# A POOL fill and a wait on its signal behind every gather of a graph convolution

## The chip, the cores and the metric

One Trainium2 chip, one core. The metric is the device time of one execution in microseconds (us); the kernel before takes 2434.01 us (median of 3 runs, 2430.92 to 2440.19).

## What is computed

One edge convolution over a graph of 6250 nodes with 64 channels and 200,000 edges sorted by destination, then a residual and a layer norm. In the reference, cut:

```python
mean = jnp.mean(x, axis=0)
var = jnp.mean(jnp.square(x - mean), axis=0)
xn = (x - mean) * rsqrt(var + 1e-5) * gamma + beta
feat = jnp.concatenate([xn[dst], xn[src] - xn[dst]], axis=-1)
h = relu(feat @ W1 + b1)            # 200000 x 128
msg = h @ W2 + b2                   # 200000 x 64
agg = segment_max(msg, dst, 6250)   # 0 where a node has no edge
agg = relu(jnp.where(isfinite(agg), agg, 0.0))
out = layernorm(x + agg)            # over the 64 channels
```

## The kernel before

The first layer is linear, so it is split over the two ends of an edge: a table `a_dram` holds each node's share as a destination and `b_dram` (128 floats a node) its share as a source. The edges are cut in two halves that run side by side, each in 196 steps of 512 edges (`NI = 196`, `GE = 512`). The sources' rows come in two ways. For 28 steps (`picked`) PE selects them by matmuls with one-hot matrices (`select`, L1146 and L1153), whose tiles are spread over all steps, and DVE makes the one-hots (`node_onehot`, L919). For the other 168 steps POOL gathers them with indirect DMAs of 128 rows each, eight to a step (four tiles, two halves): for the first 12 such steps 64 channels out of `x` (`gather`, L494; the first one needs four), 92 gathers, and for 156 steps 128 channels out of `b_dram` (`gather_wide`, L511), 1248 gathers.

What orders the work is written out by hand: each engine has its own program, and semaphores tie them together.

- POOL: a few constants (L478 to L486; L480 waits for L478's signal), then the 92 narrow gathers back to back, then the wide ones. The first wide one waits until `b_dram` is written. Wide gathers go into a ring of eight buffers (`NXB = 8`): group i waits for `wide_ps`, the signal that PE has transposed group i - 8; groups 2 to 7 wait for `x_ps`, since they lie where the narrow rows lay. At the end POOL scatters the last rows of the output (L526).
- PE, in step k of the loop: transposes of the running maxima of step k - 2 (`turn`, L1196, signal `turn_ps`), the gathered rows of the step (`rows_wide`, L1205, signal `wide_ps`), the destination's share (`hidden_dst`, L1215), the messages of step k - 1 (L1190), the sums of step k - 2 (L1234), then some tiles of the selection.
- ACT: takes what `turn` left out of PSUM (`take_rows`, L683, waits for `turn_ps`), the hidden layer's relu (L688), one-hots of the windows (L640, L644).
- DVE: picks of rows (L972, waits for `turn_ps`), one-hots for the selection (L919), the running maximum over each segment (L993, waits for PE L1190).
- SP: loads of keys and tables, stores.

Before the loop PE makes the tables (L1094), ACT and DVE split and store them (L596, L602, L826, L832), and SP writes them out.

Of the kernel before, what the change touches and what calls it, by code (L numbers as in the profile page):

```python
# [6 lines left out]
def edge_conv_program(nc, x, src, dst, gamma, beta, W1, b1, W2, b2, out):  # L7
# [13 lines left out]
    P = 128  # L21
# [66 lines left out]
    def wide_slot(i):  # L88
        return (i + NX // 2) % NXB
# [4 lines left out]
    def sides(k):  # L94
        return 1 if k == 0 else 2

    def landed(g):
        return 16 * TG * sides(gathered[g])
# [11 lines left out]
    with ctx:  # L110
        def sb(name, shape, dt=f32):
            return ctx.enter_context(nc.sbuf_tensor(name, shape, dt))
# [4 lines left out]
        def sem(name):  # L117
            return ctx.enter_context(nc.semaphore(name))
# [69 lines left out]
        cen_sq = sb("cen_sq", [P, C])  # L188
        nrm = sb("nrm", [P, 5])
        yblk = sb("yblk", [P, C])  # L190

        src_tv = src_t[:, :].rearrange("p (h b e) -> p h b e", h=2, b=NB)
        src_b = src_t[0:PN, 0:2 * GE]
# [96 lines left out]
        acc_ps, added = sem("acc_ps"), sem("added")  # L290
        end_step, end_sq, end_std, xwin_used = sem("end_step"), sem("end_sq"), sem("end_std"), sem("xwin_used")
        y_ready, y_out, tail_out = sem("y_ready"), sem("y_out"), sem("tail_out")

        g_in, g_pair_in, g_x_ps, g_x_sb = sem("g_in"), sem("g_pair_in"), sem("g_x_ps"), sem("g_x_sb")
        g_hid_ps, g_hid_sb, g_msg_ps, g_msg = sem("g_hid_ps"), sem("g_hid_sb"), sem("g_msg_ps"), sem("g_msg")
# [18 lines left out]
        def edge_tiles(eng, body):  # L314
            with eng.Fori(0, E // P) as i:
                body(i, i * P)
            if E % P:
                body(E // P, E - P)

        @block.sync  # L320
        def _(sp):
# [74 lines left out]
            def starts(ap, last):  # L396
                _, firsts = nc.values_load_multi_w_load_instructions(
                    ap, engines=[mybir.EngineType.SP], min_val=0, max_val=last,
                    skip_runtime_bounds_check_because="in_order is set only where every start lies in 0..last")
                return firsts  # L400
# [75 lines left out]
        @block.gpsimd  # L476
        def _(pool):
            pool.memset(ident[:, :], 0.0).then_inc(consts_ready, 1)  # L478
            pool.wait_ge(consts_ready, 1)
            pool.affine_select(out=ident[:, :], in_=ident[:, :], compare_op=ALU.not_equal, fill=1.0, base=0,  # L480
                               pattern=[[-1, P]], channel_multiplier=1).then_inc(consts_ready, 1)
            pool.iota(slot_row[:, :], pattern=[[1, SL]], base=1, channel_multiplier=0,
                      allow_small_or_imprecise_dtypes=True).then_inc(consts_ready, 1)
            pool.iota(slot_rep[:, :], pattern=[[1, SL], [0, NPC]], base=1, channel_multiplier=0,
                      allow_small_or_imprecise_dtypes=True).then_inc(consts_ready, 1)
            pool.iota(part_col[:, :], pattern=[[0, 1]], base=0, channel_multiplier=1,  # L486
                      allow_small_or_imprecise_dtypes=True).then_inc(consts_ready, 1)

            def gather(g):
                k = gathered[g]  # L490
                b, q = divmod(k * TG, SB)
                for t in range(TG):
                    for h in range(sides(k)):
                        pool.indirect_dma_start(xs[:, g, t, h, :], None, x[:, :],  # L494
                                                bass.IndirectOffsetOnAxis(ap=src_ix[:, b, q + t, h:h + 1], axis=0))\
                            .then_inc(rows_in[g], 16)

            def gather_wide(i):
                k = gathered[NX + i]
                u = wide_slot(i)  # L500
                if i == 0:
                    pool.wait_ge(b_first, 32)
                    pool.wait_ge(b_out, 32 * (AG - 1))
                if i >= NXB:
                    pool.wait_ge(wide_ps, i - NXB + 1)
                elif i >= NXB - NX // 2:
                    pool.wait_ge(x_ps, 2 * u + 2)
                b, q = divmod(k * TG, SB)
                for t in range(TG):
                    for h in range(2):  # L510
                        pool.indirect_dma_start(xb[:, u, t, h, :], None, b_dram[:, :],  # L511
                                                bass.IndirectOffsetOnAxis(ap=src_ix[:, b, q + t, h:h + 1], axis=0))\
                            .then_inc(wide_in[u], 16)

            pool.wait_ge(src_ix_ready, 2)
            for g in range(NX):
                gather(g)
            pool.wait_ge(flag_ready, 1)
            windowed = pool.value_load(in_order[0:1, 0:1], min_val=0, max_val=1)
            with pool.If(windowed == 1):  # L520
                pool.wait_ge(src_ix_ready, 5)
                for i in range(len(gathered) - NX):
                    gather_wide(i)

                def scatter(p):
                    pool.indirect_dma_start(out[:, :], bass.IndirectOffsetOnAxis(ap=tail_ix[0:ROWS, p:p + 1], axis=0),  # L526
                                            y[:, p, :], None, bounds_check=N - 1, oob_is_err=False).then_inc(tail_out, 16)

                pool.wait_ge(tail_ready, 1)
                pool.wait_ge(y_ready, LB // WB + 1)  # L530
                pool.wait_ge(y_out, 32 * LB)
                for p in range(WB - 2):
                    scatter(p)
                for p in range(WB - 2, WB):
                    pool.wait_ge(y_ready, len(GROUPS) - WB + p + 1)
                    scatter(p)
            with pool.Else():
                for u in range(NX):
                    pool.wait_ge(rows_in[u], landed(u))

                def edge_tile(i, first):
                    loaded = pool.to_reg(i * 48 + 48)
                    pool.wait_ge(src_ix_ready, 2)
                    pool.wait_ge(g_in, loaded)
                    for side in range(2):
                        pool.indirect_dma_start(pair[:, side, :], None, x[:, :],
                                                bass.IndirectOffsetOnAxis(ap=pair_ix[:, side:side + 1], axis=0)).then_inc(g_pair_in, 16)

                edge_tiles(pool, edge_tile)
# [787 lines left out]
```

## Time and profile before

| | us |
|---|---|
| median of 3 runs | 2434.01 |
| span of the profiled execution | 2422.7 |
| PE matmul busy in it | 1818.5 (75%) |
| DVE busy | 1292.7 (53%) |
| POOL busy | 1283.2 (53%) |
| ACT busy | 862.0 (36%) |
| mean granted TensorE clock | 0.878 |

The span runs from the first to the last instruction of the profiled execution; the page gives no other time of its own for that execution. A busy engine in these rows has an instruction running; time in which it waits for a signal is idle. In a timeline a bracket behind an instruction says how long its engine had been idle and what ended that; "remote" or "unknown queue" means that no instruction ends at the time of the signal. A gather on POOL ends in these rows when its descriptors are written, not when the rows have landed.

### The profile page before, as it was taken

What the parts mean: (1) busy time and instruction counts of PE and PEld (TensorE: products, weight loads), DVE (VectorE), ACT (ScalarE), POOL (GpSimd) and SP (SyncE); (2) the same over time, 40 slices, a digit from 0 to 9 for tenths busy, and PEclk for the clock granted to TensorE, in tenths of its full rate; (3) what the DMA queues carried; (4) which work ended last, traced back from release to release, by engine and by line L of the source; (5) the groups of instructions that cost most, each with busy time, mean ns of one, the idle gap of its engine ahead of it and who ended that gap; (6) DMA issues with size and microseconds to landing.
All of it is one profiled execution on the core that took longest, in us unless ns stands there. A gap on an engine that the chain in (4) does not pass through costs nothing.

```text
span 2422.7 us, 31826 instructions
## 1 busy us (share of the span) xinstructions
PE 1818.5 (75%) x12305; PEld 938.5 (39%) x12305; DVE 1292.7 (53%) x2070; ACT 862.0 (36%) x968; POOL 1283.2 (53%) x1356
## 2 busy tenths in 40 slices
PE   2046887787878778787878878878788778887785
PEld 1032444343434434343434444444444434444443
DVE  2054655565555555555555556556456555565553
ACT  2044443333333333333333333333334333333333
POOL 7715245556555565456555565555655565555621
PEclk6557899998999999898989899998999988898996
DMA  4154223233333332333323333233323333333320
GB/s 93 35 173 122 59 84 81 77 90 86 80 86 84 88 95 70 85 81 96 87 70 91 87 87 80 81 89 95 89 72 94 91 81 81 75 94 87 76 62 5
DMA packets 132832, 202.31 MB, mean 84 GB/s; under 512 B 74828, under 2 KB 76937, under 8 KB 132648
## 3 DMA queue, kind: packets, MB, share of 16 engines
q0 software_dynamic: 43440, 85.03, 16.5%
q1 hardware_dynamic: 87946, 115.04, 14.9%
q8 instruction: 97, 1.59, 0.3%
q10 hardware_dynamic: 1294, 0.20, 0.1%
q14 instruction: 55, 0.45, 0.1%
HBM read 189.19 MB, written 12.60 MB: 83 GB/s over the span
## 4 chain that ended last, share of the span: by engine, by line
another core or an unknown queue 38%; PE 29%; ACT 19%; issue 8%; DVE 5%; DMA 1%; SPq 0%; POOLq 0%; DVEq 0%; ACTq 0%
PE ps_g L1146 10%; PE ps_g L1153 6%; ACT hid L688 5%; ACT best L640 5%; PE ps_mr L1190 4%; ACT best L644 4%; ACT best L683 3%; PE ps_acc L1234 2%; DVE oh L919 2%; PE ps_h L1205 2%; PE ps_mr L1196 2%; PE ps_h L1215 1%; DVE runmax L993 1%; PE ps_h L1222 1%
## 5 line engine op out<-in xcount | busy, mean ns | idle before, releaser
L511 POOL DMA_INDIRECT xb<-b_dram,src_ix x1248 | 1181.1, 946 | 1031.4 <-PE ps_h L1205 384.9
L919 DVE TENSOR_SCALAR oh<-ps_k 128x1024 bf16<-128x1024 bf16 x1372 | 849.6, 678 | 1.0
L1146 PE MATMUL ps_g<-oh,xtab 128*128 128x512 bf16 x2744 | 643.5, 387 | 5.8 <-issue 5.0
L1190 PE MATMUL ps_mr<-hid,w 128*64 128x512 f32 x784 | 270.8, 776 | 369.9 <-ACT best L683 325.6
L972 DVE TENSOR_TENSOR best<-ps_acc,last_key 128x336 f32<-128x336 f32 x196 | 99.3, 507 | 815.8 <-remote 655.9
L683 ACT ACTIVATE best<-ps_mr 128x512 f32<-128x512 f32 x196 | 117.0, 597 | 1097.1 <-remote 816.3
L1146 PEld LDWEIGHTS ps_g<-oh,xtab 128*128 128x128 bf16 x2744 | 256.9, 99 | 375.6 <-issue 103.3
L1153 PE MATMUL ps_g<-oh,xtab 128*64 128x512 bf16 x2744 | 387.1, 424 | 12.6 <-issue 11.3
L993 DVE TENSOR_TENSOR_SCAN runmax<-rb,runmax,ps_mr 128x512 f32<-128x512 bf16 x196 | 249.6, 1274 | 97.4 <-PE ps_mr L1190 55.1
L688 ACT ACTIVATE hid<-ps_h,bias 128x1024 f32<-128x1024 f32 x196 | 217.9, 1112 | 106.8 <-remote 42.2
L1190 PEld LDWEIGHTS ps_mr<-hid,w 128*64 128x64 f32 x784 | 44.1, 154 | 479.6 <-ACT best L683 391.8
L1153 PEld LDWEIGHTS ps_g<-oh,xtab 128*64 128x64 bf16 x2744 | 168.0, 124 | 156.9 <-issue 68.2
L644 ACT ACTIVATE best<-best,ones 126x1024 bf16<-126x1024 bf16 x196 | 225.1, 1148 | 6.4
L640 ACT ACTIVATE best<-kb,minus_key 126x1024 bf16<-126x1024 bf16 x196 | 224.2, 1144 | 0.0
L1234 PEld LDWEIGHTS ps_acc<-best 128*42 128x42 f32 x3136 | 150.3, 148 | 163.4 <-issue 152.1
L1205 PE MATMUL ps_h<-ident,xb 128*128 128x128 f32 x1248 | 172.3, 277 | 25.2 <-issue 24.9
L1234 PE MATMUL ps_acc<-best 128*42 128x65 f32 x3136 | 159.2, 258 | 1.9 <-DVE best L972 1.1
L1205 PEld LDWEIGHTS ps_h<-ident,xb 128*128 128x128 f32 x1248 | 144.1, 142 | 29.5 <-issue 29.3
L1196 PE MATMUL ps_mr<-ident,runmax 128*128 128x128 f32 x784 | 122.7, 279 | 9.2 <-DVE runmax L993 7.1
L1215 PE MATMUL ps_h<-best,aw 126*128 126x512 bf16 x392 | 123.0, 392 | 8.6 <-issue 7.3
L1196 PEld LDWEIGHTS ps_mr<-ident,runmax 128*128 128x128 f32 x784 | 97.2, 143 | 56.5 <-issue 17.2
L494 POOL DMA_INDIRECT xb<-in_x,src_ix x92 | 89.3, 971 | 30.5 <-issue 27.7
(181 smaller groups left out, 537.2 us busy)
## 6 DMA issues: line engine op xcount, KB each, us to landing
kb<-keys_dram SPq DMA_DIRECT2D x98, 504.0 KB
rb<-reset_dram SPq DMA_DIRECT2D x98, 256.0 KB
xb<-b_dram,src_ix POOLq DMA_INDIRECT x1248
src_t<-in_src SPq DMA_DIRECT2D x56, 256.0 KB
aw<-a_dram SPq DMA_DIRECT2D x196, 31.5 KB
a_dram<-oh SPq DMA_DIRECT2D x6, 672.0 KB, 3.5
xwin<-xp_dram SPq DMA_DIRECT2D x196, 10.5 KB
out<-y SPq DMA_DIRECT2D x182, 10.5 KB
```

What stands on the lines that cost most here:

```text
L511: pool.indirect_dma_start(xb[:, u, t, h, :], None, b_dram[:, :], bass.IndirectOffsetOnAxis(ap=src_ix[:, b, q + t, h:h + 1], axis=0))\
L640: act.activation(onehot[:, k % 2, :, :], kb[0:SR, s, :].rearrange("p (h e) -> p h e", h=2)[:, :, i * GE:(i + 1) * GE], ACT.Abs, bias=minus ...
L644: act.activation(onehot[:, k % 2, :, :], onehot[:, k % 2, :, :], ACT.Relu, bias=ones[0:SR, 0:1], scale=-1.0).then_inc(onehot_ready, 1)
L688: act.activation(hid[:, k % 2, :, :], ps_h[:, :, :], ACT.Relu, bias=bias1[:, :]).then_inc(hid_sb, 1)
L919: dve.tensor_scalar(oh[0:PN, n % NOH, :], node_keys_ps, n % TN + 0.5, None, ALU.is_equal).then_inc(oh_ready, 1)
L993: dve.tensor_tensor_scan(runmax[:, (k - 1) % 2, :], rb[:, s, i * GE:(i + 1) * GE], ps_mr[:, :], runmax[:, k % 2, GE - 1:GE], ALU.add, ALU. ...
L1146: last = pe.matmul(ps_g[:, h, :], xtab[0:PN, t, 0:2, :].rearrange("p w c -> p (w c)"), oh[0:PN, n % NOH, h * GE:(h + 1) * GE], start=t == ...
L1153: pe.matmul(ps_g[h * C:(h + 1) * C, h, :], xtab[0:PN, n % TN, 2, :], oh[0:PN, n % NOH, h * GE:(h + 1) * GE], start=False, stop=False)
L1190: last = pe.matmul(ps_mr[h * C:(h + 1) * C, :], w2[:, :], hid[:, j % 2, h, :], start=True, stop=True)
L1196: last = pe.transpose(ps_mr[:, t * P:(t + 1) * P], runmax[:, j % 2, t * P:(t + 1) * P], ident[:, :])
L1205: last = pe.matmul(ps_h[:, h, t * P:(t + 1) * P], xb[:, u, t, h, :], ident[:, :], is_transpose=True, start=t == 0, stop=False)
L1234: last = pe.matmul(ps_acc[h * 64:h * 64 + SL, p * C1:(p + 1) * C1], pick[:, j % 2, t * 2 + h, :], rows[:, j % 2, t * 2 + h, :], start=(i = ...
```

## The change

After each indirect gather, narrow or wide, POOL fills a 128x1 scratch tile, the fill raises a semaphore, and POOL waits for that semaphore before it goes on. The scatters at the end have none.

```diff
+        spacer = sb("spacer", [P, 1])
...
+        spaced = sem("spaced")
...
+            handshakes = [0]
+
+            def space():
+                pool.memset(spacer[:, :], 0.0).then_inc(spaced, 1)
+                handshakes[0] += 1
+                pool.wait_ge(spaced, handshakes[0])
+
             def gather(g):
...
                         pool.indirect_dma_start(xs[:, g, t, h, :], None, x[:, :],
                                                 bass.IndirectOffsetOnAxis(ap=src_ix[:, b, q + t, h:h + 1], axis=0))\
                             .then_inc(rows_in[g], 16)
+                        space()
 
             def gather_wide(i):
...
                         pool.indirect_dma_start(xb[:, u, t, h, :], None, b_dram[:, :],
                                                 bass.IndirectOffsetOnAxis(ap=src_ix[:, b, q + t, h:h + 1], axis=0))\
                             .then_inc(wide_in[u], 16)
+                        space()
```

## Rows read from the trace of the kernel before

**Rows 1.** The page: chain that ended last by engine; groups of the gathers (busy, mean ns, idle before).

```profile
another core or an unknown queue 38%; PE 29%; ACT 19%; issue 8%; DVE 5%; DMA 1%; SPq 0%; POOLq 0%; DVEq 0%; ACTq 0%
...
L511 POOL DMA_INDIRECT xb<-b_dram,src_ix x1248 | 1181.1, 946 | 1031.4 <-PE ps_h L1205 384.9
...
L494 POOL DMA_INDIRECT xb<-in_x,src_ix x92 | 89.3, 971 | 30.5 <-issue 27.7
```

**Rows 2.** Waits, whole span: who waited for whom, total us, times, longest.

```profile
ACT best L683 <- remote: 816.3, 120, 8.5
...
POOL xb L511 <- remote: 195.1, 96, 2.2
```

**Rows 3.** Timeline, 937 to 945 us: start, duration, instruction, [idle before, releaser].

```profile
937.26 0.60 PE L1196 MATMUL ps_mr<-ident,runmax 128*128 128x128 f32 x4
...
937.70 1.04 PE L1205 MATMUL ps_h<-ident,xb 128*128 128x128 f32 x8
...
939.25 0.94 POOL L511 DMA_INDIRECT xb<-b_dram,src_ix  x1 [0.30 <-issue]
...
942.10 0.60 ACT L683 ACTIVATE best<-ps_mr 128x512 f32<-128x512 f32 x1 [8.06 <-remote]
942.43 0.94 POOL L511 DMA_INDIRECT xb<-b_dram,src_ix  x1 [2.24 <-remote]
...
942.75 1.97 PE L1190 MATMUL ps_mr<-hid,w 128*64 128x512 f32 x4 [3.09 <-ACT best L683]
...
944.77 1.28 DVE L993 TENSOR_TENSOR_SCAN runmax<-rb,runmax,ps_mr 128x512 f32<-128x512 bf16 x1 [0.37 <-PE ps_mr L1190]
```

**Rows 4.** Timeline ahead of the loop, 5 to 131 us.

```profile
5.38 1.13 POOL L494 DMA_INDIRECT xb<-in_x,src_ix  x1 [2.79 <-DVE src_ix L773]
...
45.70 0.27 PE L1094 MATMUL ps_g<-w_ab,best 64*128 64x128 f32 x1 [1.47 <-issue]
...
82.11 0.60 ACT L596 ACTIVATE oh<-ps_x 128x512 bf16<-128x512 f32 x1 [41.05 <-remote]
...
121.51 0.94 POOL L494 DMA_INDIRECT xb<-in_x,src_ix  x1 [0.30 <-issue]
...
130.41 0.60 ACT L596 ACTIVATE oh<-ps_k 128x512 bf16<-128x512 f32 x1 [46.34 <-remote]
```

**Rows 5.** Timeline, the run of 24 wide gathers, 173 to 209 us.

```profile
173.64 0.95 POOL L511 DMA_INDIRECT xb<-b_dram,src_ix  x1 [51.19 <-DMA b_dram<-xb]
...
186.34 1.98 PE L1190 MATMUL ps_mr<-hid,w 128*64 128x512 f32 x4
...
208.03 1.28 DVE L993 TENSOR_TENSOR_SCAN runmax<-rb,runmax,ps_mr 128x512 f32<-128x512 bf16 x1 [29.65 <-remote]
```

**Rows 6.** Timeline, the run of five scatters, 2396 to 2405 us.

```profile
2396.66 1.60 POOL L526 DMA_INDIRECT out<-y,tail_ix  x1 [61.72 <-issue]
...
2398.55 1.58 POOL L526 DMA_INDIRECT out<-y,tail_ix  x1 [0.30 <-issue]
...
2403.24 1.06 PE L1215 MATMUL ps_h<-best,aw 126*128 126x512 bf16 x2
...
2404.34 1.11 ACT L688 ACTIVATE hid<-ps_h,bias 128x1024 f32<-128x1024 f32 x1 [4.33 <-PE ps_h L1215]
```

**Rows 7.** Timeline after POOL's last gather, 2336 to 2402 us.

```profile
2336.72 0.60 ACT L683 ACTIVATE best<-ps_mr 128x512 f32<-128x512 f32 x1 [7.98 <-remote]
...
2363.89 0.59 ACT L683 ACTIVATE best<-ps_mr 128x512 f32<-128x512 f32 x1
...
2401.48 1.97 PE L1205 MATMUL ps_h<-ident,xb 128*128 128x128 f32 x8
```

**Rows 8.** Timeline of POOL's first instructions.

```profile
0.26 0.10 POOL L1327 MEMSET const-float32-0.0<- 128x1 f32 x1 [0.26 <-issue]
...
0.75 0.20 POOL L478 MEMSET ident<- 128x128 f32 x1 [0.29 <-POOLq L1327]
1.20 0.28 POOL L480 TENSOR_SCALAR_AFFINE_SELECT ident<-ident 128x128 f32<-128x128 f32 x1 [0.25 <-POOL ident L478]
```

## The prediction

> **What bounds the kernel now.** The page first. TensorE (PE) is the busiest engine, with 75% of the span (the table above), yet the longest share of the chain that ended last, 38%, is put down to "another core or an unknown queue" [rows 1]. There is one core, so this is time in which an engine waited for a signal whose sender had, by the records, finished long before. The table of waits says who waits so: ACT at L683, which waits for PE's transposes at L1196, 120 times and 816.3 us in all; and POOL at L511, 96 times, 195.1 us, so 2.03 us each [rows 2]; for another 384.9 us POOL waits at L511 in the ordinary way, for PE to free a buffer [rows 1].
>
> Next the timeline of one step. PE's transposes of L1196 end at 937.26 + 0.60 = 937.86. They raise the signal on which ACT L683 waits, and ACT is idle, but it starts at 942.10, 4.2 us late. PE's transposes at L1205, which free a buffer for POOL, end at 938.74; POOL starts its next gather at 942.43 [rows 3]. What lies between is POOL's run of eight gathers: the last one ends at 939.25 + 0.94 = 940.19, and ACT starts 1.91 us later. I read this as: **while POOL issues gathers back to back, signals of PE are held up, and they pass only when the run is over.** PE's next matmul (L1190) waits for ACT, so PE stands still until 942.75.
>
> The stages before the loop show it larger. PE finishes the first tables at 45.97; ACT, which waits for them, starts at 82.11 and again at 130.41, and the last of the 92 narrow gathers ends at 122.45 [rows 4]. Nothing else works there. The run of 24 gathers from 173.64 to 203.31 does it too: PE L1190 ends at 188.32 and the scan that waits for it starts at 208.03 [rows 5].
>
> Two rows bound the effect. Early in a run the signal is prompt: PE L1190 ends at 944.72, 2.3 us after the run's first gather, and the scan starts at 944.77 [rows 3]. And in the run of five scatters at the end, which has the same 0.30 us gap but a stride of 2398.55 - 2396.66 = 1.89 us, PE L1215 ends at 2404.30, 7.6 us into the run, and ACT L688 starts at 2404.34 [rows 6]. At that point of a run of gathers the signal would be late. So a backlog that builds up over some gathers at a stride of 1.25 us, and does not at 1.89, fits better than a gather being in flight as such.
>
> So the loop is a ring today: PE's signal frees a buffer, POOL runs 8 x 0.946 + 7 x 0.30 = 9.67 us of gathers [rows 1, 3], PE's signals are held until some 2 us later, and only then both go on: 9.67 + 2.03 = 11.7 us a step. With POOL silent a step takes (2363.89 - 2336.72) / 3 = 9.06 us [rows 7].
>
> **The change part by part.** Removed: nothing. Moved: nothing. Added behind each of 92 + 1248 gathers [rows 1]: a fill of 128x1 on POOL, its signal, and a wait on POOL. Only later gathers (and L526's scatters) are queued behind the wait on POOL; no other engine waits for that signal. SP's and ACT's queues aren't touched.
>
> The price of one handshake. A gather is 0.946 us [rows 1] and the next starts 0.30 us behind it [rows 3], stride 1.246. The new stride is gather + gap to the fill + fill + gap behind a waited signal. The last term is in the trace: L478 fills, L480 waits for it on the same engine, and the idle time is 0.25 us; I take 0.26 [rows 8]. A fill is 0.10 us (one column) to 0.20 us (128 columns) [rows 8]; I take 0.12, being near the first. The gap between a gather and a fill isn't in the trace: between nothing (the fill is queued and may follow at once) and the 0.30 us that a gather needs; I take 0.20, since part of that 0.30 is a gather's own start. Stride: 0.946 + 0.20 + 0.12 + 0.26 = **1.526 us**, between 0.946 + 0 + 0.10 + 0.25 = 1.30 and 0.946 + 0.30 + 0.20 + 0.26 = 1.71. So 0.28 us is added 1340 times: 375 us of POOL's time.
>
> [...]
>
> What the 375 us lie beside. Today POOL waits for PE 384.9 + 195.1 = 580 us at L511 [rows 1, 2]. If the signals stayed late, the price would lie on the path all the same, since they are late because the run is long. If they become prompt, PE doesn't wait for POOL's run to end: up to eight groups are buffered, POOL and PE work side by side, and the longer of the two sets the time.
>
> POOL: first gather at 5.38 [rows 4], then 1340 x 1.526 = 2045 us without a stop, 1.9 us until the last rows have landed (the same 1.91 as above), and what follows the last group, from 2401.48 (its transposes) to the end at 2422.7: 21.2 us [rows 7]. Sum 5.4 + 2045 + 1.9 + 21.2 = **2074 us**.
> PE: the stage ahead of the loop, which today ends with the wide gathers' start at 173.64 [rows 5], could end some 85 us sooner (41 + 46 us of ACT's two waits, less 2 us that they would last anyway [rows 4]), so at about 88; 196 steps of 9.06 are 1776; with 20 us behind, **1884 us**. So PE is 190 us ahead over the whole, and what is late next is POOL: it becomes the bound, and PE waits for landed rows. The wide gathers can't start before b_dram is written (those 173.6 us today, about 88 then); the narrow ones end at 5.4 + 92 x 1.526 = 146, so that wait falls away.
>
> The span is 2422.7; the median of the runs is 2434.01, so 11.3 us lie around the span (the profiled execution has no time of its own on the page). 2074 + 11 = **2085**. With the stride at its ends: 1.71 gives 5.4 + 2291 + 23 + 11 = 2330; 1.30 gives less than PE needs, so 1884 + 11 = 1895.
>
> **The rivals.**
> *Signals stay late (slower).* What holds PE's signals may be that gathers are in flight, or POOL's traffic as such, and 0.28 us more between two gathers may be too little to let them through. Then a group of eight is 8 x 0.28 = 2.2 us longer, and each step with it: 96 to 148 steps (those with the 2 us wait, or all groups but the first eight), 211 to 327 us, and 92 x 0.28 = 26 us ahead of the loop: 2670 to 2790, middle 2730. It decides if the held signals need a pause longer than about 0.5 us, or a stride somewhere between 1.53 and 1.89. For it: the same hold comes in runs of 8, 24 and 92 gathers. Against: the prompt signals 2.3 us into a run, and those among the scatters [rows 3, 6].
>
> The Trainium skill (VectorE: DVE Perf Modes, section "The TRN2 errata — SBUF-src ops pay a fixed extra latency per instruction") warns that dense completion signals of several engines can block another engine and advises to space them. By that rule the 1340 new signals could worsen the hold, which is this rival and its time, as well as the new gaps could end it. The late signals of PE in this trace agree with the warning; nothing here shows that POOL's own signals matter.
>
> *POOL's own signal is held (slower).* The fill's signal comes right after a gather. If it waits as PE's does at a run's end, 1.91 us, the stride is 0.95 + 1.91 + 0.10 + 0.26 = 3.22 us and the time 5.4 + 4315 + 23 + 11, about 4350. Against: after one or two gathers PE's signals are prompt.
> *The handshake is dearer.* Break-even is a stride of (2422.7 - 5.4 - 23.1) / 1340 = 1.787 us, 0.54 us above today's. A fill that waits for more of the gather than I assume could cost that: a stride of 1.79 to 1.95 gives 2434 to 2650.
> *The change does nothing* to the signals and its price is hidden: POOL's 580 us of waits would cover 375: 2434. But those waits exist only because of the late signals.
>
> **Chances.** Forecast, signals prompt and POOL the bound: 0.72 (own range 1895 to 2330). Signals stay late: 0.11. Own signal held: 0.06. Dearer handshake: 0.08. Nothing: 0.03. A measurement of this kernel tells some 0.5% from no change. Faster 0.73, same 0.03, slower 0.24. The range runs from 1895 to 2450, which takes in the forecast, no change, and the near edge of the dearer handshake; the two far rivals, 0.17, and its far end are left out.
>
> **What the profile would show.** POOL at L511: stride 1.53 (1.30 to 1.71), no idle time put down to PE after the first groups. ACT L683 starting within 0.1 us of the end of PE L1196 also in the middle of a group. "Another core or an unknown queue" no longer the first of the chain, POOL in its place. No empty stretch between 46 and 130 us: ACT L596's waits of 41 and 46 us gone. Loop steps of about 10.5 us on average, and PE waiting at L1205. The prediction is wrong if ACT L683 still waits until POOL's group has ended, or if the fill's start or signal comes over 0.5 us later than assumed.

## The result

The changed kernel takes 2499.73 us (median of 4 runs, 2472.34 to 2505.1) against 2433.34 us (4 runs, 2430.92 to 2440.19) of the kernel before: ratio 1.0239, 95% interval 1.0198 to 1.028. It is **slower by 2.4%**, where 2085 us and a gain of 14% were forecast. That nothing changed is ruled out; that the loss is a full 2% is not quite shown, since the interval begins at 1.0198. The span of its profiled execution, the longest of the four, is 2503.1 us, 80.4 us more than before's 2422.7; between the medians lie 66.4 us.

The kernel before itself took 2417 to 2444 us in some of the sessions and 1711 to 1720 us in the others, and one and the same chip met both (one chip in the first and third session, another in the second and fourth), so every run below is compared with the kernel before in its own session: the first kind is called *late* here and the second *prompt*, after PE's signals in them.

The page of the changed kernel: the chain by engine, then the groups of the wide gathers and of the fills (L521 answers to before's L511).

```profile
PE 42%; another core or an unknown queue 31%; ACT 13%; issue 9%; DVE 5%; ACTq 0%; POOL 0%; DVEq 0%; POOLq 0%
...
L521 POOL DMA_INDIRECT xb<-b_dram,src_ix x1248 | 1183.8, 949 | 967.1 <-PE ps_h L1216 407.6
...
L494 POOL MEMSET spacer<- 128x1 f32 x1340 | 152.4, 114 | 1.0
```

"Another core or an unknown queue" is still there, 31% where it was 38% [rows 1], and POOL isn't in the chain. The waits of the changed kernel over the whole span (ACT L694 was L683):

```profile
ACT best L694 <- remote: 742.0, 93, 14.7
...
POOL xb L521 <- PE ps_h L1216: 407.6, 45, 18.2
...
POOL xb L521 <- remote: 151.9, 75, 2.9
```

ACT waits 742.0 us for PE's signals where it waited 816.3 [rows 2]; a little is gone, the ring is not. Taken start by start, 103 of the 196 starts of ACT L694 are *late* (ACT was idle and started more than 0.2 us behind the end of PE's transposes), by 3.6 us on average, and 81 of them fall in a pause of POOL; in the kernel before it was 131 starts, 3.4 us and 123. One step in the timeline (start, duration, instruction, idle time before it):

```profile
902.17 0.60 PE L1207 MATMUL ps_mr<-ident,runmax 128*128 128x128 f32 x4
...
903.43 0.95 POOL L521 DMA_INDIRECT xb<-b_dram,src_ix  x1 [0.27 <-issue]
...
904.37 0.11 POOL L494 MEMSET spacer<- 128x1 f32 x1
...
905.83 0.60 ACT L694 ACTIVATE best<-ps_mr 128x512 f32<-128x512 f32 x1 [8.70 <-remote]
...
906.63 0.95 POOL L521 DMA_INDIRECT xb<-b_dram,src_ix  x1 [2.15 <-PE ps_h L1216]
...
907.58 0.11 POOL L494 MEMSET spacer<- 128x1 f32 x1
...
907.96 0.94 POOL L521 DMA_INDIRECT xb<-b_dram,src_ix  x1 [0.27 <-POOL spacer L494]
```

This is [rows 3] again. PE's transposes end at 902.77, ACT starts at 905.83, 3.06 us late and 1.45 us after POOL's last gather has ended (904.38; before 1.91). And it shows the price of a handshake: the fill starts at 907.58, when the gather ends (906.63 + 0.95), takes 0.11, and the next gather comes 0.27 behind it: stride 907.96 - 906.63 = **1.33 us**, not 1.53.

Ahead of the loop some of the hold is gone:

```profile
132.77 0.94 POOL L503 DMA_INDIRECT xb<-in_x,src_ix  x1 [0.27 <-issue]
133.72 0.11 POOL L494 MEMSET spacer<- 128x1 f32 x1
137.34 0.60 ACT L631 ACTIVATE xb<-ps_x 128x512 f32<-128x512 f32 x1 [25.40 <-remote]
...
150.94 1.34 POOL L521 DMA_INDIRECT xb<-b_dram,src_ix  x1 [17.10 <-DMA b_dram<-xb]
```

The longest silence of ACT is 25.40 us instead of 41 and 46, and the wide gathers start at 150.94 in place of 173.64 [rows 4, 5]: 22.7 us gained. From there to the end the changed kernel needs 2503.1 - 150.94 = 2352.2 us, before 2422.7 - 173.64 = 2249.1: 103.1 more. The new price alone is 156 groups x 8 gathers x (1.331 - 1.249) = 102 us, paid on top of the hold, because that still mostly lasts until the group has ended. That the two agree to 1 us is in part luck: up to POOL's last gather the difference is 114.6 us, and what follows it is 11.5 us shorter (76.3 against 87.8).

### The profile page after: what moved, and what is told of

It is laid out like the page before. It is cut to its first block, busy times and chain, and to the rows that moved or that the text cites. A ratio compares the mean times of both kernels' runs of the same rounds, so it can differ in the third digit from the quotient of the medians.

```text
span 2503.1 us, 33134 instructions
## 1 busy us (share of the span) xinstructions
PE 1862.2 (74%) x12117; PEld 953.0 (38%) x12305; DVE 1294.2 (52%) x2070; ACT 866.3 (35%) x968; POOL 1438.8 (57%) x2696
## 3 DMA queue, kind: packets, MB, share of 16 engines
q0 software_dynamic: 43440, 85.03, 16.1%
## 4 chain that ended last, share of the span: by engine, by line
PE 42%; another core or an unknown queue 31%; ACT 13%; issue 9%; DVE 5%; ACTq 0%; POOL 0%; DVEq 0%; POOLq 0%
PE ps_g L1157 14%; PE ps_g L1164 9%; PE ps_mr L1201 5%; ACT hid L699 3%; PE ps_h L1216 3%; ACT best L651 3%; ACT best L655 3%; PE ps_mr L1207 3%; PE ps_acc L1245 2%; PE ps_h L1226 2%; ACT best L694 2%; DVE oh L930 2%; PE ps_h L1233 1%; DVE runmax L1004 1%
## 5 line engine op out<-in xcount | busy, mean ns | idle before, releaser
L521 POOL DMA_INDIRECT xb<-b_dram,src_ix x1248 | 1183.8, 949 | 967.1 <-PE ps_h L1216 407.6
L1157 PE MATMUL ps_g<-oh,xtab 128*128 128x512 bf16 x2556 | 630.7, 390 | 98.9 <-issue 94.7
L694 ACT ACTIVATE best<-ps_mr 128x512 f32<-128x512 f32 x196 | 116.9, 597 | 1138.3 <-remote 742.0
L1201 PE MATMUL ps_mr<-hid,w 128*64 128x512 f32 x784 | 257.1, 739 | 301.0 <-ACT best L694 243.2
L1164 PE MATMUL ps_g<-oh,xtab 128*64 128x512 bf16 x2744 | 418.6, 429 | 56.3 <-issue 52.2
L1245 PEld LDWEIGHTS ps_acc<-best 128*42 128x42 f32 x3136 | 143.0, 141 | 152.7 <-issue 139.4
L1216 PE MATMUL ps_h<-ident,xb 128*128 128x128 f32 x1248 | 179.7, 285 | 22.1 <-issue 21.4
L1216 PEld LDWEIGHTS ps_h<-ident,xb 128*128 128x128 f32 x1248 | 150.5, 147 | 32.5 <-issue 32.3
L1245 PE MATMUL ps_acc<-best 128*42 128x65 f32 x3136 | 151.6, 250 | 2.0 <-DVE best L983 1.1
L494 POOL MEMSET spacer<- 128x1 f32 x1340 | 152.4, 114 | 1.0
L1207 PE MATMUL ps_mr<-ident,runmax 128*128 128x128 f32 x784 | 133.3, 291 | 21.9 <-issue 16.6
L1226 PE MATMUL ps_h<-best,aw 126*128 126x512 bf16 x392 | 128.5, 408 | 8.6 <-issue 8.2
```

Source lines behind the costliest of these rows:

```text
L1157: last = pe.matmul(ps_g[:, h, :], xtab[0:PN, t, 0:2, :].rearrange("p w c -> p (w c)"), oh[0:PN, n % NOH, h * GE:(h + 1) * GE], start=t == ...
L1164: pe.matmul(ps_g[h * C:(h + 1) * C, h, :], xtab[0:PN, n % TN, 2, :], oh[0:PN, n % NOH, h * GE:(h + 1) * GE], start=False, stop=False)
L1201: last = pe.matmul(ps_mr[h * C:(h + 1) * C, :], w2[:, :], hid[:, j % 2, h, :], start=True, stop=True)
L1207: last = pe.transpose(ps_mr[:, t * P:(t + 1) * P], runmax[:, j % 2, t * P:(t + 1) * P], ident[:, :])
L1216: last = pe.matmul(ps_h[:, h, t * P:(t + 1) * P], xb[:, u, t, h, :], ident[:, :], is_transpose=True, start=t == 0, stop=False)
L1245: last = pe.matmul(ps_acc[h * 64:h * 64 + SL, p * C1:(p + 1) * C1], pick[:, j % 2, t * 2 + h, :], rows[:, j % 2, t * 2 + h, :], start=(i = ...
```

## Experiments

The hunk that most of them change, in the changed kernel:

```diff
+        spacer = sb("spacer", [P, 1])
...
+            def space():
+                pool.memset(spacer[:, :], 0.0).then_inc(spaced, 1)
+                handshakes[0] += 1
+                pool.wait_ge(spaced, handshakes[0])
```

**The theories.** A: it is the distance between gathers that lets PE's signals through, and 1.33 us is too little. B: the signals are held by gathers in flight as such, or by POOL's new signals, and no distance of this size helps.

### First session: widths, count, wait, place

It was a prompt one: the kernel before took 1714.18 us (13 runs, 1711.47 to 1719.7). Nothing was held in it, so its four runs can't decide between A and B; they show what each spacing costs.

**e1_fill256**: a wider fill.

```diff
-        spacer = sb("spacer", [P, 1])
+        spacer = sb("spacer", [P, 256])
```

> The changed kernel with a fill of 256 columns in place of one, so that the gathers' stride becomes about 1.53 us (1.33 measured, plus some 0.2), the one that the prediction assumed. Theory A (rate: PE's signals are held only while gathers come faster than some backlog drains, and 1.33 is still too fast): the signals are prompt, POOL is the bound, 5 + 1340 x 1.53 + 34 = about 2090 us. Theory B (any run of gathers holds them, whatever the stride): 148 steps are 8 x 0.2 us longer, about 2500 + 240 + 18 = 2755 us.

Measured: 2132.9 us (one run), stride 1.547.

**e2_two_handshakes**: fill, signal and wait twice.

```diff
-                pool.memset(spacer[:, :], 0.0).then_inc(spaced, 1)
-                handshakes[0] += 1
-                pool.wait_ge(spaced, handshakes[0])
+                for _ in range(2):
+                    pool.memset(spacer[:, :], 0.0).then_inc(spaced, 1)
+                    handshakes[0] += 1
+                    pool.wait_ge(spaced, handshakes[0])
```

> The changed kernel with two fills and two waits behind each gather: stride about 1.33 + 0.385 = 1.72 us. Theory A (rate): 5 + 1340 x 1.72 + 34 = about 2345 us, with POOL never waiting for PE in the loop. Theory B (any run of gathers): 2500 + 148 x 8 x 0.385 + 35 = about 2990 us.

Measured: 2100.09 us (one run), stride 1.48:

```profile
900.21 0.94 POOL L522 DMA_INDIRECT xb<-b_dram,src_ix  x1 [0.27 <-POOL spacer L495]
901.16 0.27 POOL L495 MEMSET spacer<- 128x1 f32 x2
901.70 0.94 POOL L522 DMA_INDIRECT xb<-b_dram,src_ix  x1 [0.27 <-POOL spacer L495]
```

Both fills lie within 0.27 us, and the stride is 1.49 in these rows: the second handshake costs some 0.15 us, where this run's forecast had 0.385. The 0.27 us ahead of a gather comes once, however many waits stand before it: it is the start of the gather and not the price of the wait.

**e3_fill_no_wait**: the fills without the wait; so that they are free of each other each has its own column.

```diff
-        spacer = sb("spacer", [P, 1])
+        spacer = sb("spacer", [P, 1340], mybir.dt.uint8)
...
-                pool.memset(spacer[:, :], 0.0).then_inc(spaced, 1)
+                pool.memset(spacer[:, handshakes[0]:handshakes[0] + 1], 0).then_inc(spaced, 1)
                 handshakes[0] += 1
-                pool.wait_ge(spaced, handshakes[0])
```

> The changed kernel without the wait: each fill writes a byte column of its own (so no two fills write the same place) and still signals, and POOL doesn't wait. If only the stride counts: it falls to 1.25 to 1.33 us and the time lies between 2434 and 2500 us, with the steps as long as 8 strides + 2 us. If the wait itself does something to PE's signals (POOL's queue is empty for a moment), they are later here than with it, and the stretch ahead of the loop is as long as in the kernel before (wide gathers from 173 us on, not 151).

Measured: 1714.4 us, ratio 1.0001 (0.9988 to 1.0015).

```profile
900.57 0.12 POOL L494 MEMSET spacer<- 128x1 uint8 x1
900.87 0.94 POOL L520 DMA_INDIRECT xb<-b_dram,src_ix  x1 [0.19 <-issue]
901.81 0.12 POOL L494 MEMSET spacer<- 128x1 uint8 x1
902.12 0.94 POOL L520 DMA_INDIRECT xb<-b_dram,src_ix  x1 [0.19 <-issue]
```

The stride is 902.12 - 900.87 = 1.25 as before: the fill fits into the gap of 0.30 us that a gather has ahead of it anyway. The whole price of the change is its wait.

**e4_wide_only**: handshakes behind the wide gathers alone (`space()` taken out of `gather`).

> The handshake behind the 1248 wide gathers only, none behind the 92 narrow ones ahead of the loop. If the loop's longer runs of gathers are where the change loses (0.085 x 8 us a step, 148 steps, 100 us) and the earlier start of the loop (151 in place of 173 us) is what it gains: 2500 + 23 = about 2523 us. If the loss lay in the narrow stage: about 2434 us.

Measured: 1830.42 us, ratio 1.0679 (1.0655 to 1.0703). Of the price here nearly all belongs to the wide gathers.

### Second session: what is different here

It was prompt too: the kernel before 1716.95 us (7 runs, 1714.3 to 1719.92). **f1_kernel_before** is the kernel before with a profile, **f2_changed** the changed kernel, both without an edit; **f3_fill128** has `[P, 128]` for the fill, **f4_fill256_again** `[P, 256]`.

> The kernel before, unchanged, for a profile of it on the chip of this call. In the last call's runs the kernel before took 1714.18 us, in the first profile's 2434.01. Theory A (there are two regimes, with the chip, not with the kernel: in one PE's signals are held during runs of gathers, in the other they aren't): beside a time near 1714 us ACT L683 starts within 0.1 us of PE L1196's end everywhere, POOL never waits for PE and is the bound (1340 x 1.249 + 34 = 1708 us); beside a time near 2434 us the trace is like the first one. Theory B (the first profile's waits are the profiler's or a bad reading of mine): the late signals are in this trace too, whatever the time.

> The changed kernel. If the kernel before takes about 1714 us beside it, POOL is the bound in both and only the stride counts: 1340 x (1.331 - 1.249) = 110 us more, 1824 us, ratio 1.064. If the kernel before takes about 2434 us beside it: 2472 to 2505 us as before, ratio 1.024. If the handshake cost more than its stride (theory C: its signals disturb others), it is over 1850 us in the first case.

> The changed kernel with a fill of 128 columns: stride about 1.42 us. Where signals aren't held: POOL the bound, 1340 x 1.42 + 34 = 1937 us. Where they are held: if a stride of 1.42 is enough to let them through, also about 1940 us, far below the kernel before; if not, 2434 + 148 x 8 x 0.17 = about 2650 us.

> The fill of 256 columns once more (stride 1.547 us, 2132.9 us where the kernel before took 1714 us). Where signals aren't held: 2133 us again. Where they are held and a stride of 1.55 lets them through: about 2133 us too, below the kernel before. Where they are held and it doesn't: 2434 + 148 x 8 x 0.30 + 27 = about 2815 us.

Measured: f1 1714.19; f2 1840.1, ratio **1.0718** (1.0698 to 1.0737); f3 1991.22; f4 2132.89 us. The page of f1, PE's busy time and the chain, and its first two lines of waits:

```profile
PE 1631.2 (95%) x12305; PEld 876.7 (51%) x12305; DVE 1293.0 (76%) x2070; ACT 872.1 (51%) x968; POOL 1286.3 (75%) x1356
...
PE 91%; ACT 2%; DVE 2%; SPq 2%; DMA 1%; issue 1%; ACTq 1%; POOLq 0%; DVEq 0%
...
ACT best L683 <- PE ps_mr L1196: 519.6, 157, 5.0
POOL xb L511 <- issue: 379.1, 1244, 0.3
```

Compare [rows 1, 2]: the same instructions, the same gathers of 0.948 us at a stride of 1.25, but no "unknown queue" in the chain and no wait of ACT L683 on "remote"; its waits are for PE's work. PE is busy for 95% of the span, and POOL's gathers follow one another without a pause (no idle time over 0.31 us) until the last one ends at 1686.6, 25.5 us before the end: both are at their limit, so whatever lengthens POOL's run shows in the time. This is what the prediction expected of prompt signals, without any change. In the changed kernel f2 POOL is the bound, and still never waits for PE:

```profile
POOL 48%; PE 33%; issue 13%; DMA 2%; SPq 1%; DVE 1%; ACT 1%; ACTq 1%; POOLq 0%; DVEq 0%
...
POOL xb L521 <- POOL spacer L494: 335.7, 1226, 0.6
```

So where signals are prompt the change costs more, 7.2%: 5 + 1340 x 1.327 = 1783 us are POOL's start and its gathers, 19.8 us follow (the prediction had 23.1), and of the other 34 us of the span of 1837.4 some 23 are 31 gaps longer than 0.27 us. With no signal late there is nothing for the distance to gain.

### Third session: four widths in one kernel

**g1_four_widths**: 256 columns behind each narrow gather; behind the wide ones, an eighth of the groups each, nothing, 1, 128 and 256 columns, and that order once more.

```diff
+            def space(columns):
+                if columns == 0:
+                    return
+                pool.memset(spacer[:, 0:columns], 0.0).then_inc(spaced, 1)
...
+                        space(256)
...
+                        space((0, 1, 128, 256)[i * 8 // 156 % 4])
```

> One kernel with four spacings in turn, so that one profile shows them all: behind the wide gathers no fill, a fill of 1, of 128 and of 256 columns (strides 1.249, 1.331, 1.44, 1.547 us), each for 19 or 20 groups and then all four once more; 256 columns behind the narrow gathers. Where PE's signals aren't held (kernel before near 1714 us): POOL the bound in each stretch, 142 + 312 x (1.249 + 1.331 + 1.44 + 1.547) + 39 = about 1918 us, and groups as long as 8 strides. Where they are held (kernel before near 2434 us): theory A (rate) has ACT L694's late starts in the first two stretches and none in the last two, and groups of 14.0, 14.5, 11.5 and 12.4 us, some 2255 us in all; theory B (any run of gathers) has late starts in all four, groups of 14.0, 14.5, 15.5 and 16.4 us, about 2570 us.

Measured: 2303.86 us against 2443.5 (one run each), a late session. ACT's waits for PE's late signals, in the four first sections (none, 1, 128, 256 columns; windows 153 to 441, 441 to 700, 700 to 986 and 987 to 1225 us):

```profile
ACT best L696 <- remote: 77.7, 12, 8.1
...
ACT best L696 <- remote: 113.2, 14, 15.0
...
ACT best L696 <- remote: 84.8, 8, 12.2
...
ACT best L696 <- remote: 18.8, 3, 7.3
```

At strides of 1.25, 1.33 and 1.44 us the signals are held; at 1.55 much less. Counted start by start, ACT was late by 48.9, 49.9, 54.9 and 11.3 us in all in these four sections, and by 94.5 (52.6 of them a single start), 53.6, 58.0 and 16.1 us in the four that follow. The groups took 14.4, 13.6, 14.3 and 12.5 us ((1224.8 - 986.9) / 19 for the last, by the gathers that open the sections): the widest fill had the *shortest* groups, 8 x 1.547 = 12.4, so POOL hardly waited. Theory B had no place for that; theory A had none for the section at 1.44, where it expected no late start and groups of 11.5 us. But sections follow one another and can lend each other buffered groups, so it needed a kernel with one width.

### Fourth session: one width, in a late session

The kernel before took 2423.47 us (13 runs, 2418.86 to 2434.11). **h1_fill256** is e1_fill256 again, **h2_spaced_narrow_only** has the fill of 256 columns and `space()` in `gather` alone, **h3_no_wait** is e3_fill_no_wait again.

> The changed kernel with a fill of 128x256 in place of 128x1, behind narrow and wide gathers alike; stride 1.547 us. If the kernel before takes about 2440 us here (PE's signals held): theory A, a longer distance between two gathers relieves the ring even though single signals are still late. The section at this stride of the kernel with four widths took 12.4 us a group, so 156 x 12.4 = 1934, from a start near 153 and 34 us behind it: about 2120, faster than before by 13%. Rival B, that section was only living off groups buffered in the cheaper sections: then the groups are 8 x 0.3 = 2.4 us longer than before's 13.6 and the time is about 2700. If the kernel before takes about 1715 us here, both expect 2133 again.

> Fill of 128x256 and wait behind the 92 narrow gathers only, none behind the wide ones. If signals are held here: the wide gathers start near 151 in place of 173.6 and the rest goes as before, so 20 us less than before, about 0.8%. Rival: the loop takes that gain back, no difference. If they are not held (before about 1715): the narrow stage ends at 5 + 92 x 1.547 = 147 in place of 124, so 20 to 25 us slower.

> The changed kernel without its wait: each fill has a column of its own (uint8), and POOL doesn't wait for its signal. If signals are held here: theory A, it is the distance between gathers that counts, and without the wait the stride is 1.249 as before, so the time is before's within 0.5%, 2434 to 2443. Rival: the 1340 more signals worsen the hold of PE's signals, and the time is over 2460. If they are not held: the time of the kernel before, within 0.5%.

Measured: **h1 2135.52 us, ratio 0.8809** (0.8785 to 0.8833); h2 2367.3, ratio 0.9759 (0.973 to 0.9787); h3 2421.02, ratio 0.9989 (0.9967 to 1.001).

h1's page (chain) and its waits; "remote" is nowhere among its waits. (The table puts 68 more of ACT's waits, 223.7 us, down to "issue"; start by start, none of ACT's 162 waited starts there comes more than 0.04 us behind the end of PE's transposes.)

```profile
POOL 73%; issue 16%; PE 5%; DMA 1%; SPq 1%; DVE 1%; ACTq 0%; ACT 0%; POOLq 0%; DVEq 0%
...
ACT best L694 <- PE ps_mr L1207: 347.5, 94, 6.2
...
POOL xb L521 <- POOL spacer L494: 274.2, 1003, 0.6
```

And in its timeline, in the middle of a run of gathers that never pauses:

```profile
943.04 0.60 PE L1207 MATMUL ps_mr<-ident,runmax 128*128 128x128 f32 x4
...
943.67 0.60 ACT L694 ACTIVATE best<-ps_mr 128x512 f32<-128x512 f32 x1 [3.86 <-PE ps_mr L1207]
...
943.78 0.33 POOL L494 MEMSET spacer<- 128x256 f32 x1
...
944.38 0.95 POOL L521 DMA_INDIRECT xb<-b_dram,src_ix  x1 [0.27 <-POOL spacer L494]
```

PE ends at 943.64, ACT starts at 943.67. In [rows 3] the same signal came 4.2 us late. This is the mechanism of the prediction at work: signals prompt, POOL the bound. Its sum has the right form too: with the measured price a gather costs 0.951 + 0.325 for the fill + 361.0 / 1248 = 0.289 idle, 1.565 us on average, and 5.4 + 1340 x 1.565 + 23.1 = 2126 against a span of 2129.3; POOL's own instructions fill the span. In the prompt session the same kernel took 2132.9: at this stride the two kinds of session give the same time. The granted clock is the same there as well (0.912 in h1, 0.906 in f4), though it is 0.878 against 0.982 for the kernel before.

h2 gains 56 us where 20 were expected: it starts its wide gathers at 153.24, 20 us earlier than before's 173.64, and the other 36 lie in the loop; why is left open. h3 keeps the 1340 new signals and drops the distance (stride 1.25), and nothing changes:

```profile
ACT best L693 <- remote: 804.2, 117, 8.5
```

So POOL's own signals neither help nor worsen the time. The changed kernel (held) and h1 (not held), both timed in late sessions, differ in nothing but the width of the fill, so it is what the wider fill adds, the distance, that ends the hold.

### Fifth to seventh session: where the hold ends

The fifth was prompt (the kernel before 1715.22 us, 7 runs). **i1_fill192** has `[P, 192]`, **i2_two_handshakes** is e2 again, **i3_fill128** f3 again, and **i4_every_second** pauses twice as long behind every second gather:

```diff
-        spacer = sb("spacer", [P, 1])
+        spacer = sb("spacer", [P, 224])
...
+            asked = [0]
...
             def space():
-                pool.memset(spacer[:, :], 0.0).then_inc(spaced, 1)
-                handshakes[0] += 1
-                pool.wait_ge(spaced, handshakes[0])
+                asked[0] += 1
+                if asked[0] % 2:
+                    return
+                for _ in range(2):
+                    pool.memset(spacer[:, :], 0.0).then_inc(spaced, 1)
+                    handshakes[0] += 1
+                    pool.wait_ge(spaced, handshakes[0])
```

> The changed kernel with a fill of 128x192: by the fills of 128 and 256 columns (0.219 and 0.326 us) a fill of 0.272 and a stride of 1.494 us. If PE's signals are held here for the kernel before (about 2440): theory A, the hold ends where the stride passes a point between 1.44 and 1.547; if the point is below 1.494, POOL is the bound and the time is 5 + 1340 x 1.494 + 51 = about 2060 (51: what h1_fill256 had over its own 1340 x 1.547 + 5, by its 2129); if it is above, ACT still waits over 300 us for signals of unknown origin and the time is over 2200. If they are not held (before about 1715): 5 + 2002 + 55 = 2060 as well.

> Two handshakes of one column each behind every gather; stride 1.483 us, by e2_two_handshakes. If signals are held here: if only the distance between gathers counts, the result lies on one line with the fills of 128 (1.441) and 192 columns (1.494): 2045 to 2110 if the point is below 1.48. Rival: each POOL signal adds to the hold (now 2680 of them), then it is slower than both neighbours, 2300 or more, while the fill of 192 columns is near 2060. If not held: 2100 as e2.

> A fill of 128x128, stride 1.441 us, behind all gathers. If signals are held here: in the kernel with four widths the two sections of this stride took 14.3 and 13.4 us a group with ACT waiting 94 and 85 us for late signals, so the hold was hardly less: about 25 + 153 + 156 x 13.8 = 2330. If one relieved section helps the next (in the uniform kernel of 256 columns no late signal was left, in its sections in the mixed one some were), then POOL is the bound: 5 + 1931 + 51 = 1990. If not held: 1991 as f3.

> Two fills of 128x224 with a wait each, behind every second gather only: stride 1.249 and some 1.86 in turn, mean about 1.555 us. If signals are held here: if the mean rate of gathers counts, the hold is gone and the time is about 2140, as with 256 columns behind each (2135). Rival: each short gap between two gathers counts, or the pause must come behind each one: ACT still waits for late signals, over 2250. If not held: 5 + 1340 x 1.555 + 50 = about 2140 too.

Measured: 2061.1 (ratio 1.2018), 2101.69 (1.2257), 1991.89 (1.1617) and 2161.25 us (1.2604). In a prompt session each only pays for its stride (i4 21 us more than forecast), so these told nothing about the hold. Whether a mean rate or each single gap counts, and whether two short fills do as well as a wide one, wasn't tried in a late session.

**j1_fill192_again**, i1 again, met a late session (the kernel before 2422.97 us, 3 runs, 2417.53 to 2435.96):

> The fill of 128x192 once more (stride 1.494 us). If the kernel before takes about 2440 here (PE's signals held): theory A with its point below 1.494: 2061 as where nothing is held, and no late signals in the table of waits; with its point above 1.494: over 2200 and ACT waiting over 300 us for signals of unknown origin. If it takes about 1715: 2061.

Measured: **2061.06 us** (2 runs), ratio **0.8497** (0.8418 to 0.8577), the fastest kernel of the late sessions. Its chain and its waits:

```profile
POOL 68%; issue 16%; PE 10%; SPq 1%; DVE 1%; DMA 1%; ACT 1%; ACTq 0%; POOLq 0%; another core or an unknown queue 0%; DVEq 0%
...
ACT best L694 <- PE ps_mr L1207: 353.9, 91, 6.2
...
ACT best L694 <- remote: 210.1, 41, 8.6
```

At 1.494 us the hold isn't gone, but it is weaker: 88 of ACT's 164 waited starts are over 0.2 us late, by 1.8 us on average (before: 131, by 3.4) and 5.6 at most, and 83 of them come in the middle of a run:

```profile
932.80 0.60 PE L1207 MATMUL ps_mr<-ident,runmax 128*128 128x128 f32 x4
...
934.14 0.95 POOL L521 DMA_INDIRECT xb<-b_dram,src_ix  x1 [0.27 <-issue]
...
935.55 0.60 ACT L694 ACTIVATE best<-ps_mr 128x512 f32<-128x512 f32 x1 [2.18 <-remote]
935.63 0.95 POOL L521 DMA_INDIRECT xb<-b_dram,src_ix  x1 [0.27 <-issue]
```

PE ends at 933.40, ACT starts at 935.55: 2.15 us, while POOL goes on with its 0.27 us gaps. POOL is the bound and PE has time to spare, so these waits cost nothing: the time is that of the prompt session to 0.1 us (i1, 2061.1). The run's forecast had the time right and expected no late signals, which is not what came.

**j2_fill128_again**, the fill of 128 columns once more, met a prompt session (1714.12 us, 7 runs):

> The fill of 128x128 once more (stride 1.441 us). If the kernel before takes about 2430 here (PE's signals held): if the hold ends below 1.441, POOL is the bound and the time is 1992 as where nothing is held; if it ends between 1.441 and 1.494, ACT waits for signals of unknown origin again, POOL's price is paid on top of the hold, and the time is over 2200 (about 2330 by the sections of this stride in the kernel with four widths). If the kernel before takes about 1715: 1992.

Measured: 1991.5, ratio 1.1619 (1.1599 to 1.1638). So a whole kernel at 1.441 us has no late session to its name; only g1's sections speak of that stride.

The runs with one spacing behind every gather together:

| behind each gather | stride, us | late session, us (ratio) | prompt session, us (ratio) |
|---|---|---|---|
| nothing | 1.25 | 2423 to 2444 | 1714 to 1717 |
| fill, no wait | 1.25 | 2421.02 (0.9989) | 1714.4 (1.0001) |
| 1 column, wait (the change) | 1.33 | 2499.73 (1.0239) | 1840.1 (1.0718) |
| 128 columns, wait | 1.44 | - | 1991.22 to 1991.89 (1.16) |
| 1 column, two waits | 1.48 | - | 2100.09 to 2101.69 (1.2257) |
| 192 columns, wait | 1.49 | 2061.06 (0.8497) | 2061.1 (1.2018) |
| 256 columns, wait | 1.55 | 2135.52 (0.8809) | 2132.89 (1.24) |

## Why the prediction was wrong

- **The reading of the profile was right in the main.** PE's signals are held while POOL issues gathers back to back. h1 takes nothing away and only puts distance between gathers, and 816 us of waits on "remote" go to none. "They pass only when the run is over" holds for the groups of eight (123 of 131 late starts) and not for the long runs: ACT's start at 82.11, after 41 us of waiting, lies within the run of 92, which ends at 122.45 [rows 4], and in the run of 24, which ends at 203.31, one came through after 10 us:

```profile
196.10 1.11 ACT L688 ACTIVATE hid<-ps_h,bias 128x1024 f32<-128x1024 f32 x1 [10.29 <-remote]
```

- **The handshake's price was mis-sized, and that decided.** The sum took 0.946 + 0.20 + 0.12 + 0.26 = 1.526; measured 0.949 + 0 + 0.11 + 0.27 = 1.33. The failed term is the gap between gather and fill, 0.20 where it is nothing: in the timeline above the fill starts at 904.37, the gather ends at 904.38. The prediction had this as its lower bound (1.30).
- **The other failed step is the overlap at that bound: any distance was taken to free the signals.** "1.30 gives less than PE needs, so 1895" supposes that any distance frees the signals. But the prediction itself had only two rows for that: held at 1.25, prompt at 1.89 [rows 3, 6]. A stride of 1.30 lies by the first of them. The two unknowns, how far the change moves the stride and how far it must be moved, were bounded one by one and never together; the range left out the case that came.
- **The rival "signals stay late" is the one that came in kind**: each group longer by 8 times the price, on top of the hold. At the measured price its sum is 156 x 8 x 0.082 = 102 us less the 22.7 us ahead of the loop, so 80, against a measured 80.4 of the spans and 66.4 of the medians; with its 0.28 a gather it gave 2670 to 2790. It put the deciding point "between 1.53 and 1.89"; it lies lower: held at 1.33 (the changed kernel), weakened at 1.49 (j1), gone at 1.55 (h1). Between j1 (1.494, 2061) and h1 (1.547, 2135) the assumed stride of 1.526 would come to about 2105 by interpolation, 1% above the forecast.
- **POOL as the next bound was right where the signals are prompt** (h1, 2126 against 2129.3). So was the stage ahead of the loop, but only there: with 256 columns ACT's first products of the loop (`best<-ps_x`, L686) start at 76 us, "about 88" having been forecast.
- **Two smaller terms were off.** PE's 1884 us by itself is too much: in f1 PE did all of its work in a span of 1712.1, at a granted clock of 0.982 (before: 0.878). And the time is 2.0 us longer than the span of the same execution (2505.1 and 2503.1), not 11.3; the prediction had set the span of one execution against the median of others.
- **The other rivals.** POOL's own signal isn't held: its waited gap is 0.27 us. The handshake was not dearer but cheaper. The Trainium skill's warning about dense completion signals (VectorE: DVE Perf Modes, section "The TRN2 errata — SBUF-src ops pay a fixed extra latency per instruction") came in two halves: spacing does end the hold, as it advises, but 1340 more signals of POOL did nothing (h3, 0.9989). The page speaks of a deadlock; here signals were only late, and that it is the same thing is not shown.

What stays open: why one and the same kernel meets late and prompt sessions. In prompt ones the prediction's whole premise is missing and every version of the change that waits costs its stride (e3, without the wait, costs nothing).

## What to carry to other kernels

A change that must cross a threshold is to be sized against the threshold and not only priced: ask which row shows the effect at the size that the change reaches, and take the two unknowns together. A memset with a wait behind an indirect gather is a cheap spacer, 0.08 us with one column, and an adjustable one (0.0008 us a column more); if a trace shows signals of "unknown origin" that mostly pass when a run of gathers is over, try a stride of 1.5 us. Before taking such a spacer in, time the kernel in several sessions: here it gains 15% in one kind and loses 20% in the other.

## What the hardware showed that was not expected

- **Signals held by dense gathers, and a distance that ends it.** At 1.25 and 1.33 us from gather to gather most of PE's late signals pass after the group, 3.4 and 3.6 us late on average; at 1.49 those that are late are so by 1.8 us, within the run; in a kernel with 1.55 throughout none is.
- **The hold outlasts the run.** After 8 gathers at 1.25 us it ends 1.91 us behind the last one (1.7 to 1.8 in the middle half of the late starts before); after 24 at 1.25, 4.7 us (203.31 to 208.03) [rows 5]; after 92, 7.96 us (122.45 to 130.41) [rows 4]; after 92 at 1.33, 3.6 us (133.71 to 137.34). It doesn't simply grow with the run: in h3, after 92 at 1.25, it is 2.4 us (132.40 to 134.85). A backlog which grows while gathers come faster than something can serve them, and doesn't form at about 1.5 us, would look like this; it is an inference, and what queues is open.
- **It is not the gathers' own transfers that queue.** In the kernel before the last packet of a wide gather's rows ends 1.31 us (median, packets counted off in order of time) behind the gather's end, and in the prompt f1, where no signal is late, 2.05 us; the 95th percentiles are 3.5 and 3.4.
- **One kernel, two times, 1715 and 2430 us, on the same chip.** The gathers themselves don't differ: they are 0.946 us long in the one and 0.948 in the other. At a stride of 1.49 or 1.55 us the difference is gone (2061.06 and 2061.1; 2135.52 and 2132.89).
- **Ahead of a gather, a wait of POOL on its own signal costs little beyond the fill**: 0.27 us lie behind it where 0.30 lie ahead of any gather, and they come once (e2: two waits, still 0.27 once); and a fill without a wait disappears in that gap (e3).
